# Per-sample products of a DLRM tower: from two array strips with two samples each to four strips with one

## What is computed

```
e = stack([tbl_f[ids[:, f]] for f in range(26)], axis=1)        # 512 x 26 x 128
combined = concatenate([e, r_dense_x[:, None, :]], axis=1)      # 512 x 27 x 128
interact = einsum('bfd,bgd->bfg', combined, combined)           # 27 x 27 per sample
z = interact[:, triu_i, triu_j]                                 # 351 per sample
h = concatenate([z, r_dense_x], axis=1)                         # 479 per sample
h = maximum(h @ W_top1 + b_top1, 0)                             # 512
h = maximum(h @ W_top2 + b_top2, 0)                             # 256
y = h @ W_top3                                                  # 1
```

## Time and profile before

| | |
|---|---|
| median of 3 runs | 112.58 us (110.67, 112.58, 112.70) |
| the profiled execution, whole | 110.61 us |
| its span, first to last instruction | 108.8 us |
| TensorE busy | 101.8 us, 94% of the span |
| VectorE busy | 80.2 us, 74% |
| ScalarE busy | 75.4 us, 69% |
| share of the span that L591 has on the chain that ended last | 13% |

### The profile page before, as it was taken

How to read it: one execution, slowest core, us unless ns; L and a number is a source line. 1 busy time by engine, 2 the same in 40 slices (tenths; PEclk the granted TensorE clock), 3 DMA queues, 4 the chain that set the end, 5 groups by cost and what they waited for, 6 DMA issues and landing times.

```text
span 108.8 us, 2593 instructions
## 1 busy us (share of the span) xinstructions
PE 101.8 (94%) x994; PEld 79.9 (73%) x994; DVE 80.2 (74%) x161; ACT 75.4 (69%) x148; POOL 62.8 (58%) x72
## 2 busy tenths in 40 slices
PE   5999999989999999999898977999999989799992
PEld 1447567655766656688577967999999979798991
DVE  5599999979999999999972783489337932386210
ACT  4599379999999999999945762376527732376320
POOL 3777777777777777776777777777776000000000
PEclk9999999999999999999999999999999999999999
DMA  2854649994563817551112222122221100000000
GB/s 45 336 200 69 227 90 409 369 304 78 214 182 116 256 39 262 125 215 48 48 48 60 66 54 48 48 54 65 60 50 48 30 0 0 6 0 0 0 6 1
DMA packets 5199, 11.64 MB, mean 107 GB/s; under 512 B 1978, under 2 KB 2490, under 8 KB 5188
## 3 DMA queue, kind: packets, MB, share of 16 engines
q1 hardware_dynamic: 3120, 7.27, 20.2%
q0 software_dynamic: 2048, 4.20, 14.6%
q10 hardware_dynamic: 20, 0.02, 0.1%
HBM read 11.48 MB, written 0.00 MB: 106 GB/s over the span
## 4 chain that ended last, share of the span: by engine, by line
PE 89%; DVE 5%; issue 2%; ACT 1%; DVEq 0%
PE gram_ps L556 39%; PE gram_ps L591 13%; PE tr_ps L572 6%; PE act_ps L625 5%; PE dve_ps L625 4%; PE top_ps L636 3%; PE tr_ps L673 3%; DVE pairs L470 2%; PE dve_ps L532 2%; PE tr_ps L667 2%; PE gram_ps L532 2%; PE top_ps L660 2%; PE gram_ps L612 1%; PE tr_ps L625 1%; PE act_ps L532 1%
## 5 line engine op out<-in xcount | busy, mean ns | idle before, releaser
L280 POOL DMA_INDIRECT rows<-table,ids_sb x64 | 61.9, 967 | 20.7 <-issue 19.2
L556 PE MATMUL gram_ps<-onehot,high 128*128 128x512 f32 x82 | 23.2, 429 | 1.0 <-issue 1.0
L556 PE MATMUL gram_ps<-onehot,low 128*128 128x512 f32 x82 | 21.4, 404 | 0.0
L556 PEld LDWEIGHTS gram_ps<-onehot,high 128*128 128x128 f32 x82 | 15.3, 201 | 7.4 <-issue 3.6
L556 PEld LDWEIGHTS gram_ps<-onehot,low 128*128 128x128 f32 x82 | 14.7, 188 | 6.1 <-issue 3.4
L294 ACT ACTIVATE xt<-gram_ps 128x512 f32<-128x512 f32 x10 | 12.0, 1202 | 4.9 <-PE gram_ps L556 4.9
L591 PE MATMUL gram_ps<-xt 128*58 128x52 f32 x512 | 14.5, 217 | 0.9 <-DVE xt L429 0.6
L443 DVE TENSOR_TENSOR onehot<-dve_ps,row_f 128x1024 fp32r<-128x1024 f32 (+1 forms) x10 | 14.4, 1484 | 1.2 <-PE act_ps L532 1.2
L591 PEld LDWEIGHTS gram_ps<-xt 128*58 128x58 f32 x512 | 14.0, 133 | 1.6 <-DVE xt L429 0.8
L455 DVE TENSOR_TENSOR low<-table,high 128x256 fp32r<-128x256 f32 (+1 forms) x40 | 14.5, 426 | 0.8 <-ACT high L372 0.6
L443 DVE TENSOR_TENSOR onehot<-gram_ps,row_f 128x1536 fp32r<-128x1536 f32 (+1 forms) x10 | 14.9, 1536 | 0.0
(11 more groups left out here) (72 smaller groups left out, 106.5 us busy)
## 6 DMA issues: line engine op xcount, KB each, us to landing
table<-table SPq DMA_DIRECT2D x9, 512.0 KB, 3.9
rows<-table,ids_sb POOLq DMA_INDIRECT x64, 3.0
w1p_sb<-w_pairs SPq DMA_DIRECT2D x1, 768.0 KB, 5.6
table<-table SPq DMA_DIRECT2D x1, 640.0 KB, 4.1
w_sb<-w SPq DMA_DIRECT2D x1, 512.0 KB, 7.0
dense_sb<-dense SPq DMA_DIRECT2D x1, 256.0 KB, 4.9
w1d_sb<-w_dense SPq DMA_DIRECT2D x1, 256.0 KB, 5.9
ids_sb<-ids SPq DMA_DIRECT2D x1, 52.0 KB, 1.9
```

The costliest lines, as they stand in the source:

```text
L280: pool.indirect_dma_start(rows[:, t, s - 1, :], None, tables[f], bass.IndirectOffsetOnAxis(ids_sb[:, t, f:f + 1], 0)).then_inc(gathered[t] ...
L556: last = pe.matmul(pick_ps[b][:], weights[:, c, :], onehot[:, b, c, :], start=(c == 0 and part == 0), stop=(c == CHUNKS[o] - 1 and part == 1))
```

## The change

Each sample becomes a matmul of its own: 26 stationary columns, 26 moving ones, into the 32 partitions of its quadrant. The four samples of a group follow one another in the four strips of 32 array columns. A set is 16 groups, 64 matmuls, which fill 16 x 26 = 416 columns of a bank; a tile is two sets, in two of the three banks. So the wait of a set for a bank is gone. Each copy out of PSUM takes a whole set's 26 partitions x 416 numbers, without a gap.

```diff
@@ -58,8 +58,7 @@
 NJ = N_SLOTS - 1
-SET_G = 8
-HALF = Q // 2
+SET_G = 16
 SETS = G // SET_G
 GRAM_BANKS = 3
@@ -220,10 +219,8 @@
         def gram_block_ps(s, q):
 
-            v = gram_ps[s % GRAM_BANKS][PAD * q:PAD * q + NJ, 0:SET_G * HALF * NJ]
-            v = v.rearrange("i (g n) -> i g n", g=SET_G)
-            r = q % HALF
-            return v[:, :, r * NJ:(r + 1) * NJ].rearrange("i g j -> i j g")
+            v = gram_ps[s % GRAM_BANKS][PAD * q:PAD * q + NJ, 0:SET_G * NJ]
+            return v.rearrange("i (g j) -> i j g", g=SET_G)
@@ -583,14 +580,10 @@
                     for k in range(SET_G):
                         g = s * SET_G + k
-                        for h in range(Q // HALF):
-                            pair = xt[:, t, Q * g + HALF * h:Q * g + HALF * (h + 1), :]
-
-                            weights = pair.rearrange("d q i -> d (q i)")[:, 0:(HALF - 1) * PAD + NJ]
-                            at = h * HALF * PAD
-                            last = pe.matmul(gram_ps[s % GRAM_BANKS][at:at + (HALF - 1) * PAD + NJ,
-                                                                     k * HALF * NJ:(k + 1) * HALF * NJ],
-                                             weights, pair[:, :, 1:N_SLOTS], start=True, stop=True)
+                        for q in range(Q):
+                            sample = xt[:, t, Q * g + q, :]
+                            last = pe.matmul(gram_ps[s % GRAM_BANKS][PAD * q:PAD * q + NJ, k * NJ:(k + 1) * NJ],
+                                             sample[:, 0:NJ], sample[:, 1:N_SLOTS], start=True, stop=True)
                     last.then_inc(gram_ready, 1)
```

## The result

The changed kernel is slower: median 119.28 us over 4 runs (117.72 to 122.13), against 111.62 us over 4 runs of the kernel before (110.67 to 112.70). The ratio is 1.068, 95% interval 1.058 to 1.078. The forecast was 106.0 with a range to 118, so both direction and range missed; of the cases named, the rival "feeding" (117.8) had the sign and nearly the size. The runs of either kernel lie in clusters some 2 us apart (of before at about 108.9, 110.8 and 112.6), and the ratios compare the undisturbed runs of both sides, so they need not equal the ratio of two medians.

The account below looks back on a forecast made before the run. TensorE, busy 94% of the span, was taken as the bound. Terms of 0.88 + 1.78 + 1.78 + 0.9 = 5.3 us off 110.61 gave 105.3 by the profile, put at 106.0 for the median, range 104 to 118.

Parts of the forecast that it names:

- feeding: Rival, chance 0.30: handing the array twice as many product records binds, at 20 ns per record 117.8 us in all.
- What bounds the kernel: TensorE; shorter products count in full in tiles 1 and 2, in tiles 0 and 3 only through VectorE's last copy.
- The array's pace: In the products, four strips work side by side, paced by weight loads: 27.7 ns per strip record, 6.9 ns overall.
- a strip's turn does not shrink: Rival, chance 0.18: a strip needs 55.5 ns whatever the columns, products stay 3.55 us per tile, 111.5 us in all.
- 256 x 6.9 = 1.77 us: A tile's products: 256 records at 6.9 ns each, 1.77 us in place of 3.55.
- The range's upper bound: The upper end, 118, reaching to feeding at its nearer price: 20 ns per record, 5.1 us per tile, 117.8 us.
- Tiles 1 and 2: Products shorter by 1.78 us in each of these tiles, in full, with `back` not waiting for `packed`.
- The copies: Out of PSUM: 594 ns on VectorE, 554 on ScalarE; without gaps, ending 0.88 us sooner in tile 0, 0.9 in tile 3.
- The gathers: The last gather, landing by 86.9 us, stays hidden before the last tile's transpositions, by 1.8 us.

Follow-up runs that it names:

- e6: The changed kernel without the last tile's sixteen gathers, its rows filled with 0.25 instead; median 119.03 us.
- e4: The changed kernel with six zero matmuls of 128x512 in front of `back(0)`, where TensorE waits for `packed`; median 119.66 us.
- e1: The changed kernel with its four 128x512 warm-up matmuls replaced by 64 of 32x32, 120 more instructions at the start; 123.66 us, ratio 1.135.
- e2: The changed kernel with every second group of samples left out of the products, 64 narrow matmuls per tile for 128; median 107.33 us.
- e5: The kernel before with 16 groups of each tile as one narrow set and 16 as two wide sets; median 111.33 us, ratio 1.011.
- e3: The kernel before with each wide product matmul issued twice, 512 instructions per tile; 124.64 us.
- e7: The changed kernel with other TensorE work moved between the two sets of each tile; 121.86 us.

## Why the prediction failed, point by point

- **What bounds the kernel: right.** TensorE is the bound in tiles 1 and 2, and 1.44 and 1.25 us more products there are 1.42 and 1.21 us more between the tiles.
- **The array's pace: right as far as it goes.** 6.9 ns per record were derived for four strips; the first 32 records of a tile come 6.7 ns apart. Narrower loads do make a strip's turn shorter, so the rival "a strip's turn does not shrink" falls (it had 13.9). The 27.7 ns of before took the last record's own length into the stretch; from first to last record 3.41 us make 26.7, so a strip's turn was 53.4 and what stood on top of the load 3 ns and not 5. That moves the forecast little (1.63 in place of 1.77 us a tile).
- **The step that failed** is the product 256 x 6.9 = 1.77 us and the sentence under it, that the spacing of before "leaves nothing over for feeding". The spacing of before is set by columns; it could say nothing about feeding, which was never the slower of the two there. Measured are 4.4 to 5.1 us, in three parts: 8.3 ns in place of 6.7 after the start (a tile without a stop would take 4.65 - 2.49 = 2.16 us, tile 2), short pauses of 1.3 and 1.0 us together in tiles 0 and 1, and the long stop of 1.2 to 2.3.
- **The range's upper bound** was taken from a mean rate (20 ns per record, evenly). Its 5.1 us per tile are near what came, by another mechanism: what its own test asked for, "evenly spaced over all strips", is not what the rows show. Its argument against itself, no fast start that then slows, was looked for within before's stretch, where a block lasts 3.41 us. What should have been asked is how the instructions arrive: the page of before has 8 packets of 16 KB in the instruction queue, and the change needs four more of them, two blocks within each 1.8 us.
- **Tiles 1 and 2:** -1.78 each was forecast, +1.42 and +1.21 came. `back(1)` and `back(2)` did not wait for `packed`, as forecast.
- **The copies: the size was right, their place was not.** 593 ns for 594 on VectorE; ScalarE took 507 for 554, off its path. They were to run back to back and end 0.88 us sooner. With the sets coming slower, VectorE waits 1.93 and 2.11 us before the last set's two, and they stand bare: 1.20 in place of 0.79 us in tiles 0 and 3. The feeding rival had said just that, at 0.9 us together; 0.8 came.
- **The gathers** stayed hidden: no wait for them in front of the last transpositions. That they go with pauses in TensorE's supply (e6) was in no term.
- **The clock** was in no term. It cost 1.6 us in the profile. In e4's profile it was gone from tile 0 and came back in tile 1; one of e4's other runs had no such fall, by its mean clock.
- **The cause.** Moving the edges moves the stops (e1), half the products or the mixed form has none (e2, e5), the same count at 13.3 ns has none (e3), the refill time is not shortened by taking the gathers away (e6). That TensorE is supplied in blocks and outruns them is shown. Open is what the refill consists of: of the 3.2 to 4.0 us of all sixteen stops (after, e1, e4, e6), 0.6 to 1.6 lie ahead of the packet, 0.9 to 1.4 in it, and 1.3 to 1.6 behind it. That the sustained 8.3 ns is the supply inside a block is argued from its step after about 32 records, and was not tested by itself. Open, too, is where the limit lies exactly. Refills behind a fast block took up to 4.0 us, yet e3 has no stop at 3.41 us a block; and of the first edges in tile 2, whose blocks had lasted some 3.0 to 3.5 us (counted in steps of 256 from the stops), the changed kernel's waited not at all, e5's 0.44 us, e4's 0.46 and e7's 0.99, from record to record.

No variant that makes all the products beat the kernel before; the nearest, e5, cannot be told from it.

## What to carry to other kernels

Before splitting matmuls into more and smaller ones, count TensorE's instructions (here four per fp32 matmul, two loads and two matmuls) and compare the time in which 256 of them are used up with what a refill takes, here 3.2 to 4.0 us: a second block used up in 1.09 to 1.11 us was followed by a stop of 2.0 to 2.7 us, one used up in 1.7 to 2.3 us by 0.7 to 1.9, and at 3.41 us a block there was none. A spacing that column counts explain is no evidence of what lies behind it, since only the slower of two limits shows. And ask what a shorter stretch leaves idle: a gap can cost the clock of what follows, here 1.6 us, and the copies behind it need to be able to take the gain.

## What the hardware did that was not expected

- TensorE's instructions arrive 256 at a time; where it outran them, 3.2 to 4.0 us passed from the end of one block to the first work out of the next but one (sixteen stops in four profiles).
- Behind the first 32 records, load and matmul together take 8.3 ns at best, in place of the 6.7 of the start.
- GpSimd's gathers go with pauses of 0.20 to 0.29 us in TensorE's supply, seen with the narrow products alone (185 records in 2.83 us with gathers, 1.76 without); before, at 26.7 ns a record, has no gap above 0.15 us beside the same gathers.
- In five profiles the granted clock fell to 0.50 for 3.4 us within the tiles, once or twice (the changed kernel, e1, e2, e4, e7), each time behind idle stretches of TensorE, in e2 behind a wait for `packed` alone (1.70 us); in before, e3 and e5 it did not, and in e6 it did not either, in spite of stops of 2.08 to 2.72 us.
- At the program's start the full clock comes at about 12 or at about 16 us and moves everything behind it by 2 us. Both were seen with both kinds of kernel: 11.7 in before and 16.4 in e3, which is before with its products doubled; 16.5 in the changed kernel and 12.1 in e6, a variant of it.
